# A narrow projection as two blocks of 128x64 side by side, and a third copy made by ScalarE

## What is computed

```python
x = x + _L0_conv_ref(_gn(x), ...)   # three steps of attention, routing and a mixed 3x3 convolution
x = x + _L1_conv_ref(_gn(x), ...)   # involution

def _L1_conv_ref(x, Wr, br, gamma, beta, mean, var, Ws, bs, Wi, bi):
    r = einsum('bhwc,cd->bhwd', x, Wr) + br                      # 64 -> 16 channels
    r = relu((r - mean) * rsqrt(var + BN_EPS) * gamma + beta)
    w = einsum('bhwd,dk->bhwk', r, Ws) + bs                      # 16 -> 9 taps x 16 groups
    w = w.reshape(B, H, W, G, KK)[:, :, :, :, None, :]
    xi = einsum('bhwc,cf->bhwf', x, Wi) + bi
    patches = ...                                                # 3x3 neighbourhoods of xi, KK = 9
    out = sum(w * patches.reshape(B, H, W, G, F // G, KK), axis=-1)
    return out.reshape(B, H, W, F)
```

## Time and profile before

| | us |
|---|---|
| median of 3 runs | 698.71 (698.58 to 699.46) |
| the profiled execution | 699.03 |
| span of its trace | 697.2 |
| PE busy | 652.6 (94%) |
| DVE busy | 549.3 (79%) |
| ACT busy | 289.0 (41%) |
| POOL busy | 173.9 (25%) |
| last stage in the trace | 463 to 697 |

### The profile page before, as it was taken

How to read it: one execution, slowest core, us unless ns; L and a number is a source line. 1 busy time by engine, 2 the same in 40 slices (tenths; PEclk the granted TensorE clock), 3 DMA queues, 4 the chain that set the end, 5 groups by cost and what they waited for, 6 DMA issues and landing times.

```text
span 697.2 us, 14818 instructions
## 1 busy us (share of the span) xinstructions
PE 652.6 (94%) x6176; PEld 271.0 (39%) x6176; DVE 549.3 (79%) x896; ACT 289.0 (41%) x372; POOL 173.9 (25%) x157
## 2 busy tenths in 40 slices
PE   7878999699999999999999999979999999999993
PEld 7433333223333333333333334424444444444441
DVE  5698957968987988995565789956888888888881
ACT  3753713122322422143002410025677777777742
POOL 2100400008202800450051200212343243243241
PEclk9989999899999999999999999997999999999997
DMA  9920000000000000000000000000111211211212
GB/s 333 206 48 1 2 1 1 1 1 1 3 1 1 2 1 1 1 2 1 1 14 2 1 2 1 1 1 1 27 35 32 60 32 32 61 32 31 61 31 61
DMA packets 54478, 19.66 MB, mean 28 GB/s; under 512 B 51122, under 2 KB 51860, under 8 KB 54420
## 3 DMA queue, kind: packets, MB, share of 16 engines
q1 hardware_dynamic: 54132, 18.57, 10.9%
q10 hardware_dynamic: 288, 0.21, 0.1%
HBM read 10.39 MB, written 8.39 MB: 27 GB/s over the span
## 4 chain that ended last, share of the span: by engine, by line
PE 75%; DVE 13%; ACT 2%; issue 1%; POOL 1%; DVEq 0%; POOLq 0%; ACTq 0%
PE conv L635 36%; PE conv L711 11%; PE att L727 11%; PE att L452 5%; PE att L677 4%; DVE comb L1239 3%; DVE xpad L1158 2%; PE att L699 2%; PE conv L601 2%; PE att L689 2%; PE att L510 1%; DVE x L1215 1%; DVE x L1216 1%; DVE x L1223 1%; DVE stats L1253 1%
## 5 line engine op out<-in xcount | busy, mean ns | idle before, releaser
L635 PE MATMUL conv<-xpad,comb 64*64 64x512 f32 x2592 | 289.8, 595 | 2.8 <-DVE x L1223 2.7
L1453 DVE TENSOR_TENSOR x<-conv,x 128x512 f32<-128x512 f32 x288 | 179.3, 684 | 32.9 <-PE conv L711 31.5
L635 PEld LDWEIGHTS conv<-xpad,comb 64*64 64x64 f32 x2592 | 100.7, 134 | 168.4 <-issue 156.7
L1239 DVE SCALAR_TENSOR_TENSOR comb<-experts,wsel,comb 128x576 f32<-128x576 f32 (+1 forms) x138 | 113.7, 892 | 10.6 <-ACT comb L833 10.5
L711 PE MATMUL conv<-rstack,wse 98*128 98x512 f32 x288 | 97.0, 452 | 3.2 <-POOL rstack L1569 2.6
L833 ACT ACTIVATE comb<-experts,wsel 128x576 f32<-128x576 f32 (+2 forms) x52 | 37.2, 770 | 111.5 <-PE conv L635 69.7
L727 PE MATMUL att<-x,cmp 64*32 64x512 f32 x1280 | 79.7, 596 | 0.0
L711 PEld LDWEIGHTS conv<-rstack,wse 98*128 98x128 f32 x288 | 50.8, 194 | 61.5 <-DVE x L1453 44.4
L1158 DVE SCALAR_TENSOR_TENSOR xpad<-att,x 128x1024 f32<-128x1024 f32 x46 | 54.0, 1215 | 20.4 <-PE att L510 20.2
L1576 POOL TENSOR_TENSOR x<-x,xin 128x1024 f32<-128x1024 f32 x16 | 38.4, 2397 | 124.1 <-ACT x L973 124.1
L843 ACT ACTIVATE x<-conv,bias 128x512 f32<-128x512 f32 x40 | 25.2, 682 | 83.6 <-PE conv L635 83.6
(11 more groups left out here) (179 smaller groups left out, 602.9 us busy)
## 6 DMA issues: line engine op xcount, KB each, us to landing
x<-in_x SPq DMA_DIRECT2D x32, 256.0 KB, 5.1
out<-comb SPq DMA_DIRECT2D x32, 256.0 KB, 3.2
experts<-in_We SPq DMA_DIRECT2D x1, 1152.0 KB
wide<-in_c_wide SPq DMA_DIRECT2D x1, 192.0 KB, 5.5
x<-in_c_sum SPq DMA_DIRECT2D x1, 160.0 KB
small<-in_c_small ACTq DMA_DIRECT2D x1, 142.5 KB, 3.5
map_sel<-in_c_map SPq DMA_DIRECT2D x1, 128.0 KB
wr<-in_Wr SPq DMA_DIRECT2D x6, 4.0 KB
```

What stands on the lines that cost most here:

```text
L635: last = nc.tensor.matmul(conv[own[to], h, HW * rows:HW * rows + HW], comb[own[rows], q % 2, n, tap(t)], xpad[own[rows], 2 * (q % 2) + n, ...
L1239: v.scalar_tensor_tensor(comb[:, q % 2, n, cols], experts[:, e, cols], wsel[:, p % 2, j + QP * n, e:e + 1], comb[:, q % 2, n, cols], ALU.m ...
L1453: v.tensor_tensor(img(prod[i])[:, rows, :], img(conv[:, unit, :])[:, rows, :], xip[s][:, kh + 16 * h:kh + 16 * h + 16, kw:kw + W], ALU.mul ...
```

## The change

`wr` holds two copies of the 16 channels instead of three, 64 columns. The two halves of the pixels go into two blocks of 128x64: half 0 into `att[0:64]`, half 1 into `att[64:128]`. ACT's `empty_r` now has two Relus of 64x512, one for each half, both into `r64`; one copy of 64x1024 into rows 0 to 63 of `rstk`, and a further copy of 32x1024 into rows 64 to 95, with a semaphore of its own, `third_ready`, which expand 0 waits for as well. The batch norm's constants `rsc` cover 128 rows instead of 96. Two of the six loads of `Wr` go.

```diff
-        wr = sb("wr", [128, AR])
+        wr = sb("wr", [128, 2 * 32])
-        rpar = rpar[0:AR, :]
-        rsc = sb("rsc", [AR, 4])
+        rsc = sb("rsc", [128, 4])
-        r96 = flat[0:AR, 8 * S:9 * S]
+        r64 = flat[0:64, 8 * S:9 * S]
         BLOCKS += [(wr[64 * n:64 * n + 64, 32 * a + CR * n:32 * a + CR * n + CR], A["Wr"])
-                   for n in range(2) for a in range(PARTS)]
+                   for n in range(2) for a in range(2)]
...
-            def project(k, s, m, weights, rows):
+            def project_r(k, s, m):
                 if not (isinstance(m, int) and m == 0):
                     eng.wait_ge(misc_free, m)
                 eng.wait_ge(xn_ready, k + 1)
                 for h, cols in halves():
-                    last = nc.tensor.matmul(att[0:rows, 1, cols], weights, xn[s][:, cols], start=True, stop=True)
+                    last = nc.tensor.matmul(att[own[h], 1, cols], wr[:, :], xn[s][:, cols], start=True, stop=True)
                 last.then_inc(misc_full, 1)
...
                 if i == 0:
                     eng.wait_ge(rstk_ready, k + 1)
+                    eng.wait_ge(third_ready, k + 1)
...
-                nc.scalar.activation(r96, att[0:AR, 1, :], ACT.Relu, bias=rsc[:, 3:4], scale=rsc[:, 1:2])\
-                    .then_inc(misc_free, 1)
+                for h, cols in halves():
+                    done = nc.scalar.activation(r64[:, cols], att[own[h], 1, cols], ACT.Relu, bias=rsc[own[h], 3:4], scale=rsc[own[h], 1:2])
+                done.then_inc(misc_free, 1)
                 eng.wait_ge(misc_free, m + 1)
-                nc.scalar.activation(rstk[s][0:AR, :], r96, ACT.Copy).then_inc(rhi_ready, 1)
+                nc.scalar.activation(rstk[s][0:64, :], r64, ACT.Copy).then_inc(rhi_ready, 1)
+                nc.scalar.activation(rstk[s][64:AR, :], r64[0:32, :], ACT.Copy).then_inc(third_ready, 1)
...
-            v.tensor_tensor(rsc[:, 2:3], rsc[:, 0:1], mhalf[0:AR, 0:1], ALU.pow).then_inc(setup_pool, 1)
+            v.tensor_tensor(rsc[:, 2:3], rsc[:, 0:1], mhalf[:, 0:1], ALU.pow).then_inc(setup_pool, 1)
...
-                v.tensor_tensor(rstk[s][32:64, :], r96[32:64, :], rstk[s][32:64, :].bitcast(F32), ALU.subtract)\
+                v.tensor_tensor(rstk[s][32:64, :], r64[32:64, :], rstk[s][32:64, :].bitcast(F32), ALU.subtract)\
                     .then_inc(rstk_ready, 1)
```

More of the change, by code:

```diff
@@ L273, in build @@
         rhi_ready = sem("rhi_ready")
+        third_ready = sem("third_ready")
         rstk_ready = sem("rstk_ready")
@@ L740, in involve @@
                 if not last:
-                    project(k + 1, 1 - s, m, wr[:, :], AR)
+                    project_r(k + 1, 1 - s, m)
                 expand(k, s, 4)
@@ L753, in involve @@
                     turn_back(k - 1, m if last else m + 2)
-            project(0, 0, 0, wr[:, :], AR)
+            project_r(0, 0, 0)
             project_xi(0, 0, 1)
```

## The result

| | before | after |
|---|---|---|
| median of 13 runs, us | 698.88 (697.44 to 699.46) | 700.13 (699.07 to 701.84) |
| ratio | | 1.0020 (95%: 1.0012 to 1.0029) |
| profiled execution / span, us | 699.03 / 697.2 | 700.10 / 698.4 |
| one pair in the steady part, us | 13.01 | 13.16 |
| PE busy in 52 us of it | 52.00 | 51.42 |

The change made the kernel slower by 1.25 us, some 0.2%. The forecast was 2.6 us slower, 701.3; the direction and the mechanism held, the size was twice too large.

A forecast was written before the change was run, and what follows sets the result against it. PE was taken to bound the kernel before, a loop over ACT and PE after. 13 pairs x 0.28 = +3.7, first loop -0.3, stage's start -0.8: +2.6 on the median 698.71, so 701.3 us; range 696.5 to 705.0.

The forecast's parts named there:

- The bound: Last stage: PE busy all 52.00 us before; afterwards a loop over ACT and PE sets the pair, 13.29 against 13.01.
- PE's projection: Two 128x64 blocks side by side take 0.86 us on PE in place of 1.72; bounds 0 and 0.86 saved.
- The 0.86: PE time saved a pair by the projection's passes running side by side, 2 x 0.43 in place of 1.72.
- What PE could keep: Expand 5's last matmul waits for DVE's product: 0.36 us of 0.86 reach PE's later work, 0.50 become a wait.
- ACT's side: From `empty_sum`'s start to the transposes' weights: 9.08 us against 8.80, with two Relus of 0.77, two copies of 1.06.
- The term that was mis-sized: Transposes' first weights to the next `empty_sum`: PE's own work, unchanged at 4.21 us, making the loop 13.29.
- The stage's start: Last stage's beginning, second projection at half clock: 0.8 us gained, bounds 1.5 lost to 1.7 won.
- first loop: First to second `empty_sum` has slack, 9.42 us instead of 8.80 to the transposes' weights: gain 0.3 us.
- (1): ACT's instructions overlap at their joints: all four take 0.44 off the loop, 695.5 us; two give 698.4; chance 0.17.
- (2): ACT 0.65 us quicker, wait at `turn_back` covered, DVE's products set the pair at 13.01 - 0.36: 692.9 us; chance 0.06.
- (3): Projection's blocks not side by side: Relus start 0.29 us later, each loop +0.57, total +8.9, 707.6 us; chance 0.07.
- (4): PE's clock falls in the new waits of 0.6 us; each 10 us at 1.2 GHz costs some 4; chance 0.04.

The follow-up runs named there:

- e1: The changed kernel with ACT's third copy moved behind the four pieces of `empty_xi`, all work the same; 696.27 us, ratio to before 0.9962.
- e2: The kernel before with only its copy of 96 rows split into one of 64 and one of 32 rows; 699.99 us, ratio 1.0028.
- e4: The changed kernel with both halves of the projection in the same 64 columns of the array, one behind the other; 706.68 us, ratio 1.0114.
- e3: The changed kernel with one more 32x1024 copy on ACT behind the third, into rows nobody reads; 714.08 us, ratio 1.0221.

## Why the prediction was right or wrong

**The bound.** Right. Before, PE's records filled the pair; after, the loop from `empty_sum` over the Relus, copies, `empty_xi` and the transposes does. Taking the copy out of the loop, doubling it and adding it alone all moved the time as a loop does and not as a total.

**PE's projection.** The mechanism was right, 128x64 blocks run side by side (1.08 us against 1.93 for the same blocks in one place). The 0.86 was too much for PE itself: from the first pass to the next block's it is 544.66 - 543.65 = 1.01 us, where four passes of 0.43 took 1.72, and the first pass starts 543.65 - 542.52 = 1.13 us after expand 2's weights and not 543.66 - 542.62 = 1.04. So PE's own cut is some 0.6 us. That decided nothing, since DVE's hand-over allows less:

```profile
542.52 0.76 PEld L713 LDWEIGHTS conv<-rstack,wse 98*128 98x128 f32 x4 [0.84 <-DVE x L1457]
...
543.65 0.20 PEld L678 LDWEIGHTS att<-x,wr 128*64 128x64 f32 x4 [0.37 <-issue]
...
544.66 0.53 PEld L713 LDWEIGHTS conv<-rstack,wse 98*128 98x128 f32 x3 [0.81 <-DVE x L1457]
...
545.59 0.19 PEld L713 LDWEIGHTS conv<-rstack,wse 98*128 98x128 f32 x1 [0.41 <-DVE x L1457]
...
546.02 0.18 PEld L729 LDWEIGHTS att<-x,cmp 64*32 64x32 f32 x16 [0.24 <-issue]
```

What PE could keep was put at 0.36 and came out at 0.27. The hand-over itself came as summed: in e1 the last pass of expand 5 goes in 546.25 - 543.18 = 3.07 us after expand 2's weights, before at 546.07 - 542.62 = 3.45, 0.38 later. What was missing is the load behind the wait: that pass now has to load its weights first, and the next block's follow 546.68 - 546.25 = 0.43 us later, where they came 546.39 - 546.07 = 0.32 us after it before. The 0.11 is the difference. In the changed kernel it cost nothing, since PE waited for ACT anyway; it is what kept e1 at 12.75.

**ACT's side.** Right to 0.01 us: 9.08 forecast, 9.07 measured. (ACT's total was added up a little high, "some 11.2 of 13": 38.17 us in 52 are 9.55 a pair, and with 1.4 more 11.0; measured 11.1. Nothing hung on it.) Groups by line and form, to the earlier trace rows:

```profile
L965 ACT ACTIVATE x<-att,rsc 64x512 f32<-64x512 f32 x32 | 24.8, 775 | 6.8 <-PE att L678 6.3
...
L968 ACT ACTIVATE rstack<-x 64x1024 fp32r<-64x1024 f32 x16 | 17.0, 1059 | 0.5
L969 ACT ACTIVATE rstack<-x 32x1024 fp32r<-32x1024 f32 x16 | 16.9, 1057 | 0.4
```

The Relu of 64x512 that no row showed is 0.775 (0.77 worked out from the halved copy), and a copy of 32 rows takes as long as one of 64.

**The term that was mis-sized.** "From the transposes' weights to the next `empty_sum` it is PE's own work, 4.21 us, which the change leaves alone." It is 542.71 - 538.63 = 4.08. Before, the first transposes' weights went in while expand 8 was still streaming, and the eight took 1.09 us; behind the new wait they take 0.97, and expand 0's weights come 539.51 - 538.63 = 0.88 us after the first instead of 1.01. A wait ahead of a block of PE also takes away what that block's loads lost to the work before it. The same 4.08 stands behind the waits of e2, and 4.21 is back in e1, where nothing waits. With it the loop is 9.08 + 4.08 = 13.16 and not 13.29: 13 x 0.13 = 1.7 us of the forecast's 2.6 were this term. Without it the forecast would have been +0.9; the two traces show +0.8 in the stage, and the other 0.36 stand ahead of it. So the measured +1.25 is nearer to the forecast than the stage by itself, and that part is luck.

**The stage's start.** -0.63 against -0.8, first loop -0.25 against -0.3: right. DVE's wait behind the second projection went from 2.33 us to 1.13, and DVE waited 1.40 one step later, as the work pulled forward still ran at 1.2 GHz; the clock rose about 0.5 us later than before (0.2 later counted from the stage's first projection):

```profile
476.41 1.98 PE L678 MATMUL att<-x,wr 128*64 128x512 f32 x4
...
479.15 2.48 DVE L1457 TENSOR_TENSOR x<-conv,x 128x512 f32<-128x512 f32 x4 [1.13 <-PE conv L713]
...
480.00:481.00 1.00, 1.00 (x9) 0.23 (x16) 1.00 (x3) 0.97 (x1) 0.00 (x0) 0.50 0.00 0
```

**The rivals.** (1), overlapping joints: none of the four joints of the changed kernel overlapped; but joints that overlap exist, see below. (2), the cut reaching the end, needed ACT 0.65 us quicker; e1 took 1.08 out of the loop, and then DVE's hand-over was the bound, as that rival said, at 12.75. (3) did not happen; e4 built it, at 13.48 a pair where it had +0.57, that is 13.58. Two things made it shorter, the Relus' overlap (0.12) and the 4.08 in place of 4.21 (0.13); the Relus' start made it longer, 0.44 later than in the changed kernel and not 0.29 (0.15). (4): PE's clock stayed at 1.00 in the steady part with the waits of 0.57 us.

## What to carry to other kernels

Where two engines hand one buffer back and forth, add up the whole loop, from one instruction to the same one of the next round, and not the work of each engine: ACT had 8 us of 52 free and was still part of the bound. Work that the loop doesn't need (here a copy that ended 3.7 us before its first reader started) belongs behind the instruction that releases the other engine; that placement was worth 5.9 us of 700, where the whole change cost 1.25. At a stage's start nothing covers such a late step, so the first round may need its own order. And when a new wait lands ahead of a block whose cost is read from a trace, read that cost from a place where such a wait already stands.

## What the runs showed of the hardware that was not expected

In the last stage of all eight traces two ACT instructions in a row, the second of which waits for nothing, overlap by 0.09 to 0.11 us when neither the first source partition nor the first target partition changes between them, and not otherwise. Overlapping: the two Relus of e4 (0 to 0 twice: 1.44 us for 2 x 0.77), the third and the spare copy of e3 (0 to 64 twice, 0.09), the last piece of `empty_xi` and the third copy of e1 (0 to 64, from PSUM and from SBUF: 535.98 + 2.80 = 538.78, the copy starts at 538.67). Not overlapping: the Relus of the changed kernel (source 0, then 64), the pieces of `empty_xi` (one of the two changes at each step), the copy to row 0 followed by one to row 64. The 64-row copy behind e4's second Relu stays at 0 and 0 but waits for the Relu by a semaphore, and starts 0.03 us after its end. The Trainium skill (ScalarE: Activation LUTs, What ACT_TABLE_LOAD costs) has an overlap of about 93 ns for back-to-back ACTIVATEs; the trace agrees only where the partitions stay. Nearest to a test by itself comes the step from the changed kernel to e4: for ACT only the second Relu's source moves, from 64 to 0, and a joint of +0.01 becomes an overlap of 0.10. For the target it is e3, whose three copies all read from partition 0: from the first to the third copy the target moves from 0 to 64, with a joint of 0.02, and from the third to the spare one it stays, with the overlap.

A switch between 98x128 matmuls and blocks of 128x64 cost PE some 0.1 us at either edge: the first block starts 0.33 us after the last pass before it, where a 128x96 projection starts after 0.23, and the next expand starts 0.52 after the last pass of the blocks and not 0.43. Both halves in one block (e4) pay the same 0.33 and 0.52, and so do the 64x32 blocks of the sums, in the kernel before as well (0.32 and 0.52); so the cost goes with the change to narrower blocks and not with two blocks beside each other. The transposes (128x128) do not pay it: they start 0.24 after an expand in the kernel before. The Trainium skill (TensorEngine Tiling (Array Packing), Key Properties) says that a change of the tiling mode drains the engine; these gaps agree with it.
